# Two cross-attentions of a transformer block: 32-bit split operands become f16 and bf16 split operands

## The reference

```python
# sublayer 1: 16 heads of 64, low-rank additions to the four weights, last 4 context rows as an own attention
q_in = x @ Wq + _lora(x, q_down, q_up, q_alpha)
k_in = org_ctx @ Wk + _lora(org_ctx, k_down, k_up, k_alpha)
v_in = org_ctx @ Wv + _lora(org_ctx, v_down, v_up, v_alpha)
out = _attention(q_in, k_in, v_in)
out_ipa = _attention(q_in, ipa_ctx @ Wk_ipa, ipa_ctx @ Wv_ipa)
out = out + IPA_SCALE * out_ipa
return out @ Wo + bo + _lora(out, o_down, o_up, o_alpha)
# sublayer 3: 8 heads of 64, all 512 context rows as keys
q, k, v = x @ Wq, context @ Wk, context @ Wv
attn = softmax(q @ k.T * SCALE); return (attn @ v) @ Wout + bout
```

## Time and profile before

| | us |
|---|---|
| median of 3 runs (1086.5 to 1097.15) | 1094.68 |
| the profiled execution's own time | 1089.7 |
| its span | 1087.9 |
| stage A, steps (60 to 500 in the trace) | 440 |
| stage C, steps (757 to 962) | 205 |

### The profile page before, as it was taken

How to read it: one execution, slowest core, us unless ns; L and a number is a source line. 1 busy time by engine, 2 the same in 40 slices (tenths; PEclk the granted TensorE clock), 3 DMA queues, 4 the chain that set the end, 5 groups by cost and what they waited for, 6 DMA issues and landing times. The chain is left out here.

```text
span 1087.9 us, 23374 instructions
## 1 busy us (share of the span) xinstructions
PE 883.6 (81%) x8744; PEld 638.8 (59%) x8744; DVE 773.4 (71%) x1547; ACT 718.2 (66%) x1183; POOL 635.4 (58%) x574
## 2 busy tenths in 40 slices
PE   4887899999999999996543999968888989973476
PEld 4655676767766777775321655645566757663143
DVE  5758778777877886676667444428888887647797
ACT  3487878788878888884243343335797878952674
POOL 2177766766586667674156566542696767852143
PEclk9999999999999999997665999989798999986699
DMA  9479899899989988996492887782999889983155
GB/s 279 156 134 189 154 150 156 142 185 150 178 144 174 162 151 131 164 167 112 121 311 72 168 163 153 157 266 92 177 172 195 144 158 157 178 142 117 24 111 137
DMA packets 504879, 171.11 MB, mean 157 GB/s; under 512 B 477729, under 2 KB 495329, under 8 KB 504737
## 3 DMA queue, kind: packets, MB, share of 16 engines
q1 hardware_dynamic: 501024, 159.39, 77.1%
q0 software_dynamic: 3744, 10.23, 3.4%
HBM read 38.62 MB, written 12.71 MB: 47 GB/s over the span
## 5 line engine op out<-in xcount | busy, mean ns | idle before, releaser
L477 POOL TENSOR_TENSOR A_PHL<-A_pr,A_PHL 128x508 f16<-128x508 f32 x256 | 295.3, 1159 | 135.3 <-ACT A_pr L754 134.6
L753 ACT ACTIVATE A_PHL<-A_ps,A_negmax 128x508 f16<-128x508 f32 x256 | 179.7, 702 | 17.0 <-DVE A_negmax L1003 14.2
L477 POOL TENSOR_TENSOR C_PHL<-C_pr,C_PHL 128x512 f16<-128x512 f32 x128 | 150.2, 1183 | 58.0 <-ACT C_pr L754 57.5
L754 ACT ACTIVATE A_pr<-A_ps,A_negmax 128x508 f32<-128x508 f32 x256 | 181.6, 709 | 0.0
L1003 DVE TENSOR_REDUCE A_negmax<-A_ps 128x2 f32<-128x1016 f32 x128 | 154.2, 1205 | 0.0
L598 PE MATMUL A_ps<-A_K,A_Q 64*128 64x512 f32 x768 | 124.5, 429 | 12.6 <-ACT A_pr L754 10.5
L616 PE MATMUL A_ps<-A_VH,A_PT 128*128 128x65 bf16 (+1 forms) x1024 | 108.1, 196 | 19.8 <-DMA A_PT<-A_PHL 19.6
L616 PEld LDWEIGHTS A_ps<-A_VH,A_PT 128*128 128x128 f16 (+1 forms) x1024 | 92.9, 97 | 47.9 <-DMA A_PT<-A_PHL 28.9
L617 PE MATMUL A_ps<-A_VL,A_PT 128*128 128x64 f16 (+1 forms) x1024 | 107.1, 193 | 0.0
L618 PE MATMUL A_ps<-A_VH,A_PT 128*128 128x65 bf16 (+1 forms) x1024 | 106.8, 194 | 0.0
L753 ACT ACTIVATE C_PHL<-C_ps,C_negmax 128x512 f16<-128x512 f32 x128 | 88.8, 694 | 15.8 <-DVE C_negmax L1003 15.1
(11 more groups left out here) (344 smaller groups left out, 2517.1 us busy)
## 6 DMA issues: line engine op xcount, KB each, us to landing
A_PT<-A_PHL SPq DMA_TRANSPOSE x256, 3.3
M_raw<-in_L_ffn_w_in SPq DMA_DIRECT2D x4, 1024.0 KB, 7.7
M_raw<-in_L_ffn_w_out SPq DMA_DIRECT2D x4, 1024.0 KB, 9.4
C_yc<-routed_rows SPq DMA_DIRECT2D x8, 512.0 KB, 5.4
ct_split<-A_CT SPq DMA_DIRECT2D x4, 768.0 KB, 4.2
C_CT<-ct_split SPq DMA_DIRECT2D x4, 768.0 KB, 8.5
M_rows<-M_xhl SPq DMA_DIRECT2D x4, 512.0 KB, 8.7
out<-X SPq DMA_DIRECT2D x16, 128.0 KB, 2.0
```

Source lines behind the costliest of these rows:

```text
L477: pool.tensor_tensor(PHL[:, e % PRING, 1, 0:KEYS], pr[:, e % RING, 0:KEYS], PHL[:, e % PRING, 0, 0:KEYS], ALU.subtract).then_inc(pl_ready. ...
L753: a.activation(PHL[:, e % PRING, 0, 0:KEYS], o, ACT.Exp, bias=nm[:, n % 4, h:h + 1])
L754: a.activation(pr[:, e % RING, 0:KEYS], o, ACT.Exp, bias=nm[:, n % 4, h:h + 1]).then_inc(p_ready.sem, 1)
```

## The change

Every `FR` operand of the two attentions becomes a pair of 16-bit parts: f16 for the high part and bf16 for the low part of `WQ`, `WK`, `WV`, `WO`, `XT` and `OT`; f16 for both parts of `Q`, `K`, `KI` and for `CT`. The same products are made, in the same order. The low-rank factors stay `FR`, and so `DS` and `US` get memory of their own. The stored context is f16 and half as long (384 KB instead of 768 KB for a batch). On each of the five queues the list of instructions is the same as before, with the same shapes and waits; only operand types differ, and the names of `DS` and `US`.

```diff
-        WQ = [sb(f"WQ{s}", [P, 2, HD], FR) for s in "hl"]
-        WK = [sb(f"WK{s}", [P, 2, HD], FR) for s in "hl"]
-        WO = [sb(f"WO{s}", [P, OC, D], FR) for s in "hl"]
+        PARTS = (("h", F16), ("l", BF16))
+        WQ = [sb(f"WQ{s}", [P, 2, HD], dt) for s, dt in PARTS]
+        WO = [sb(f"WO{s}", [P, OC, D], dt) for s, dt in PARTS]
+        WK = [sb(f"WK{s}", [P, 2, HD], dt) for s, dt in PARTS]
         bias = sb("bias", [P, D], F32)
-        XT = [sb(f"XT{s}", [P, KC, N], FR) for s in "hl"]
-        CT = [sb(f"CT{k}", [P, 3, N], FR) for k in range(2 if ipa else B)]
-        Q = sb("Q", [P, SLOTS, 2, N], FR)
-        K = sb("K", [P, SLOTS, 2, N], FR)
+        XT = [sb(f"XT{s}", [P, KC, N], dt) for s, dt in PARTS]
+        CT = [sb(f"CT{k}", [P, 3, N], F16) for k in range(2 if ipa else B)]
+        Q = sb("Q", [P, SLOTS, 2, N], F16)
+        K = sb("K", [P, SLOTS, 2, N], F16)
...
-        OT = [sb(f"OT{s}", [P, 2, QT, P], FR) for s in "hl"]
+        OT = [sb(f"OT{s}", [P, 2, QT, P], dt) for s, dt in PARTS]
...
-            KI = sb("KI", [P, OC, B, 2, IPA], FR)
+            KI = sb("KI", [P, OC, B, 2, IPA], F16)
...
-        WV = [sb(f"WV{s}", [P, 2, HD], FR) for s in "hl"]
+        WV = [sb(f"WV{s}", [P, 2, HD], dt) for s, dt in PARTS]
...
-            DS = K[0:96, :, :, :].rearrange("p s a n -> p (s a n)")[:, 0:1792]
-            US = {"v": OT[0][0:96, :, :, :].rearrange("p r c n -> p (r c n)"),
-                  "k": OT[1][0:96, :, :, :].rearrange("p r c n -> p (r c n)"),
-                  "q": XT[0][0:96, :, :].rearrange("p k n -> p (k n)"),
-                  "o": CT[1][0:96, 0, 0:D]}
+            DS = sb("DS", [96, 1792], FR)
+            US = {n: sb(f"US{n}", [96, UCOLS[n]], FR)[:, :] for n in WNAMES}
...
-                sp.dma_start(scratch["ct"][b], CT[b % 2][:, :, :].bitcast(F32)).then_inc(ct_stored[b].sem, 16)
+                sp.dma_start(scratch["ct"][b], CT[b % 2][:, :, :]).then_inc(ct_stored[b].sem, 16)
...
-                                           in1=T[:, c % SLOTS, 0, 0:n].bitcast(F32), op0=ALU.mult,
+                                           in1=T[:, c % SLOTS, 0, 0:n], op0=ALU.mult,
...
-            "ct": spare("ct_split", (P, 3, N), F32),
+            "ct": spare("ct_split", (P, 3, N), F16),
```

More of the change, by code:

```diff
@@ L350, in store_ct @@
                 wait(sp, ct_split, 2 * (b + 1))
-                sp.dma_start(scratch["ct"][b], CT[b % 2][:, :, :].bitcast(F32)).then_inc(ct_stored[b].sem, 16)
+                sp.dma_start(scratch["ct"][b], CT[b % 2][:, :, :]).then_inc(ct_stored[b].sem, 16)
             def load_ct(b):
-                sp.dma_start(CT[b % len(CT)][:, :, :].bitcast(F32), scratch["ct"][b]).then_inc(ct_loaded[b].sem, 16)
+                sp.dma_start(CT[b % len(CT)][:, :, :], scratch["ct"][b]).then_inc(ct_loaded[b].sem, 16)
             def load_vwo(b):
@@ L447, in lower @@
                         last = pool.tensor_tensor(lo[:, c, :].rearrange("p c n -> p (c n)"), late[i],
-                                                  hi[:, c, :].bitcast(F32).rearrange("p c n -> p (c n)"), ALU.subtract)
+                                                  hi[:, c, :].rearrange("p c n -> p (c n)"), ALU.subtract)
                     last.then_inc(w_split.sem, 1)
@@ L451, in lower @@
                 pool.tensor_tensor(lo[:, :, :].rearrange("p c n -> p (c n)"), raw[k % 2],
-                                   hi[:, :, :].bitcast(F32).rearrange("p c n -> p (c n)"), ALU.subtract).then_inc(w_split.sem, 1)
+                                   hi[:, :, :].rearrange("p c n -> p (c n)"), ALU.subtract).then_inc(w_split.sem, 1)
             def split_ct(b):
@@ L456, in split_ct @@
                 wait(pool, ct_hi, b + 1)
-                pool.tensor_tensor(t[:, 2, :], craw[b][:, 0, :], t[:, 0, :].bitcast(F32), ALU.subtract).then_inc(ct_split.sem, 1)
+                pool.tensor_tensor(t[:, 2, :], craw[b][:, 0, :], t[:, 0, :], ALU.subtract).then_inc(ct_split.sem, 1)
                 wait(pool, ct_split, 2 * b + 1)
-                pool.tensor_tensor(t[DH:P, 1, :], craw[b][DH:P, 1, :], t[DH:P, 1, :].bitcast(F32),
+                pool.tensor_tensor(t[DH:P, 1, :], craw[b][DH:P, 1, :], t[DH:P, 1, :],
                                    ALU.subtract).then_inc(ct_split.sem, 1)
@@ L863, in low @@
                 if kind == "x":
-                    v.tensor_tensor(XT[1][:, k, :], hi_done(u), XT[0][:, k, :].bitcast(F32), ALU.subtract).then_inc(pj_free.sem, 1)
+                    v.tensor_tensor(XT[1][:, k, :], hi_done(u), XT[0][:, k, :], ALU.subtract).then_inc(pj_free.sem, 1)
                 if kind in "qk":
@@ L876, in low @@
                     v.tensor_tensor(OT[1][:, k % 2, :, :].rearrange("p c n -> p (c n)"), hi_done(u),
-                                    OT[0][:, k % 2, :, :].bitcast(F32).rearrange("p c n -> p (c n)"),
+                                    OT[0][:, k % 2, :, :].rearrange("p c n -> p (c n)"),
                                     ALU.subtract).then_inc(pj_free.sem, 1)
@@ L949, in _ @@
                 v.tensor_tensor(WV[1][:, :, :].rearrange("p c n -> p (c n)"), raw[0],
-                                WV[0][:, :, :].bitcast(F32).rearrange("p c n -> p (c n)"), ALU.subtract).then_inc(w_split.sem, 1)
+                                WV[0][:, :, :].rearrange("p c n -> p (c n)"), ALU.subtract).then_inc(w_split.sem, 1)
                 up_low("q")
@@ L956, in _ @@
                 wait(v, ipa_kvc, 1)
-                v.tensor_tensor(KI[:, :, :, 1, :], image, KI[:, :, :, 0, :].bitcast(F32), ALU.subtract).then_inc(ipa_kvc.sem, 1)
+                v.tensor_tensor(KI[:, :, :, 1, :], image, KI[:, :, :, 0, :], ALU.subtract).then_inc(ipa_kvc.sem, 1)
                 up_low("k")
```

## The result

The changed kernel takes 1059.43 us (median of 4 runs, 1058.23 to 1060.76) against 1093.38 us of the kernel before in the same set: ratio 0.971, 95% interval 0.9675 to 0.9745. It is faster by 2.9%; the forecast was 1055, its range 1034 to 1074. The profiled execution took 1058.98 us against 1089.7, which is 30.7 us less where 36.5 was forecast.

A forecast was written before the change was run, and what follows sets the result against it. TensorE's jobs were taken to bound most steps of stages A and C. Savings of 29 (A), 6 (C) and 1.5 us (v matmuls and A's opening) sum to 36.5, giving 1053.2 or 1058.2; forecast 1055, range 1034 to 1074.

The forecast's parts named there:

- What bounds: Stages A and C: most step pairs are heavy, held by TensorE's jobs; TensorE is busy 93% of A's 440 us.
- Projection jobs, scores: TensorE in both stages: q and y jobs 0.18 us less each, k and v 0.17, a score set 0.12.
- Sum of TensorE's work: TensorE's matmul work falls by 37.8 us in stage A and 16 us in stage C.
- What of it reaches the end, stage A: Stage A: 0.78 of TensorE's saving reaches the end, 29 us.
- light pairs: Pairs of steps held by ScalarE at 5.5 us, where less TensorE work gains nothing.
- The signs named beforehand: Stage A 415 us from first to last second exp, ScalarE busy 88 to 90%, its q wait half of 24 us.
- Stage C: VectorE and ScalarE hold more there, so 0.4 of 16 us passes, 6 us.
- Early takeover: Rival: ScalarE and the transposes hold the steps early; A gives 15 us, C 3, total 1072; chance 0.20.
- Drains go too: Rival: the 0.09 us gaps around scores vanish too, or more of the saving passes; total 1035; chance 0.12.
- Clock falls: Rival: TensorE idles more and its granted clock falls; at 0.88 the kernel is slower, 1102; chance 0.04.
- GpSimd's splits dearer: GpSimd's weight splits may get dearer with 16-bit parts; C's `WVl` costs 0 to +0.5 us, taken as 0.
- Context: Context stores and C's loads halve to 384 KB; transposes behind stores may come earlier: 0 to -5 us, taken as 0.

The follow-up runs named there:

- e7: The changed kernel with weigh four steps behind the scores in stage A, not three: 1039.36 us, ratio 0.963 to the kernel before, stage A 411.7 us.
- e9: The kernel before, float32r operands, with weigh four steps behind the scores in stage A: ratio 1.0039 to the kernel before, stage A 444.5 us.
- e3: The changed kernel with stage A transposing only the high parts of the probabilities, half the bytes: ratio 0.9629 to the kernel before, stage A 417.1 us.
- e4: The changed kernel with stage A's second exp on half of its columns: ratio 0.9664 to the kernel before, stage A 414.1 us.
- e2: The kernel before with only Q, K and KI as f16: 1086.67 us, ratio 0.9932 to the kernel before.
- e1: The changed kernel with Q, K and KI as float32r again, only projections and context 16-bit: 1074.22 us, ratio 0.981 to the kernel before.

## Why the prediction was right or wrong

- **What bounds.** Right: most pairs of stage A are paced by TensorE's jobs, and lighter matmuls make the whole faster, stage by stage and in each half of the change.
- **Projection jobs, scores.** Right to 0.01 us: intervals of 0.215 and 0.109 us, no 0.34 at a job's start, 0.75 us for the scores. The 0.09 around the scores stayed, as kept in the sum: 0.13 us ahead of them where weigh's matmuls are 0.03 apart, and 0.75 for the scores, which is three times 0.215 and 0.10. The Trainium skill, TensorEngine Tiling (Array Packing), Key Properties, says that a change of the tiling mode drains the engine. The rows after agree, in that the time is still there with 16-bit operands on both sides of the change.
- **Sum of TensorE's work.** Right: 35.6 and 15.3 us of busy time against 37.8 and 16.
- **What of it reaches the end, stage A.** This is the step that failed: 29 us were let through at a share of 0.78, and 18.9 passed, 0.50. The text held back light pairs and ScalarE, and put the transposed probabilities at what they cost before. What was missed is a latency. From the start of a step's scores to the landing of its last transpose pass 11.3 us at the median, before and after: by rows of the changed kernel 0.95 to the maximum, 1.20 for it, 2.4 for the four exps, 1.2 for GpSimd and 3.4 from issue to landing, 9.2 in all, and the rest in the queues of ScalarE and SyncE. Weigh's turn comes after three steps and the scores and jobs of the fourth. It started 13.0 us after the scores at the median before, and 12.4 with the shorter steps (3.33 us in the mean and not 3.48), waits for the data included. So the data were late in 50 steps and not 31, and TensorE's wait for them went from 14.1 to 29.9 us. e7 and e9 show what this costs: with four steps 32.8 us of the same saving pass, with three 18.9.
- **The total.** That 1059.4 came out 4 us beside the 1055 owes something to luck: stage A was put 10 us too high, stage C 4 too low and the rest 0.7 too low.
- **The signs named beforehand.** Missed were stage A's length (425.2 us against 415), ScalarE's busy share (366.9 of 426 us, 86%, against 88 to 90) and its wait for q (17.8 us against half of 24). All three belong to the step that failed.
- **Stage C.** 9.7 us where 6 was set, 0.61 of 16 and not 0.4. It has had a lag of four steps throughout. Why VectorE's slow stretches didn't hold back more is not shown; no run was made on that.
- **Early takeover.** This rival had 0.20 and 1072, for the reason that ScalarE and the DMA engines have no room. In stage A its 15 us lay nearer to the 18.9 than my 29 did; C's 9.7 us, where it had 3, and the total speak against it. Its reason falls as well: a lighter load on either gives 8 to 11 us (e3, e4), and e7 gets 13.5 with all of the load. Its reading of a DMA share of 0.95 as nearly full was mine as well; e7 runs at 0.99 with short waits.
- **Drains go too.** False, above. **Clock falls.** False: 0.99 and 0.94, as before, with TensorE idle 12% of stage A.
- **GpSimd's splits dearer.** The sign was wrong: `WVl` in stage C takes 2115 ns and took 2336, `WOl` in A 2127 and took 2372. It is 0.2 us each. The row of stage M that it leaned on, 2635 ns, is 2120 in e9's trace with the same types, so that the type wasn't its cause.
- **Context.** Stores of 384 KB land in 2.9 us, where 768 KB took 4.2. What this alone gives was not tried.

## What to carry to other kernels

When the bounding engine gets lighter in a pipeline of fixed step order, read the latency from producer to consumer off the trace and compare it with the time until the consumer's turn, which is the number of steps in flight times the new, shorter step and what stands ahead of the consumer in its own step. What held before may not hold any more. Here one more step in flight gave nothing before the change, and 11 to 14 us of stage A after it, beside the change's own 19. And a wait in a trace is not by itself a loss of that size: in e9 the wait for `A_PT` went, one for the exps came in its place, and the stage was as long as before.

## What the runs showed of the hardware

A float32r matmul of 512 columns costs 0.233 us where f16 or bf16 costs 0.216, so the type by itself is worth 7%. Of the 0.20 us by which a q job got shorter, the five intervals behind its first matmul give 0.09, and the first, which took 0.34 us with float32r and takes 0.23 now, gives 0.11. And the copy of 8 columns of image keys (`K` from `KI`), SBUF to SBUF on VectorE, takes no less in f16 than in 32 bits: the medians are 733 and 610 ns with f16 (the change, e2), 541 and 722 with float32r (before, e1). Its durations spread widely around the same small operand, now:

```profile
L869 DVE COPY A_K<-A_KI x31: 155/733/953, 60.6 to 465.2; 128x8 f16<-128x8 f16 x31
```

Its fastest takes 155 ns and its median 733, where the copy of the same size out of PSUM (`A_SI`) has a median of 165. Why it takes so much longer at most times was not tried.
